# A decoder layer on one core: the last batch's linear attention moved ahead of an MLP tile, and the last tiles' turned values and down projections put in other banks

## The reference

```
i, f, g = x Wi^T, x Wf^T, x Wg^T
h[t] = sigmoid(f) h[t-1] + silu(i) (1 - sigmoid(f))          # a scan over tokens
x = layernorm(x + rmsnorm(h * silu(g)) Wo^T)
x = layernorm(x + wkv(w, u, k=x, v=ctx))                     # a linear attention: decayed sums of
                                                             # exp(k) v and exp(k) over past tokens
xq = quantise rows of x to 127 levels
hid = silu(xq Wgate^T) * (xq Wup^T)                          # 2 x 1408 columns
x = layernorm(x + quantise(hid) Wdown^T)                     # Wgate, Wup, Wdown quantised too
```

## Time and profile before

| | us |
|---|---|
| median of 3 runs (434.78 to 439.98) | 437.27 |
| the profiled execution | 435.36 |
| its span, first to last instruction | 433.4 |
| mean granted TensorE clock | 0.98 |

### The profile page before, as it was taken

How to read it: one execution, slowest core, us unless ns; L and a number is a source line. 1 busy time by engine, 2 the same in 40 slices (tenths; PEclk the granted TensorE clock), 3 DMA queues, 4 the chain that set the end, 5 groups by cost and what they waited for, 6 DMA issues and landing times.

```text
span 433.4 us, 7988 instructions
## 1 busy us (share of the span) xinstructions
PE 376.4 (87%) x2810; PEld 292.3 (67%) x2810; DVE 365.8 (84%) x620; ACT 320.0 (74%) x422; POOL 234.0 (54%) x282
## 2 busy tenths in 40 slices
PE   7799889789898899889997999899989997576872
PEld 7797889687865687659764976497648774232331
DVE  3889797575998799989898988898898989899584
ACT  3687777649827898588858995799668975985571
POOL 1775554542644844766475746594459436635451
PEclk9999999989999999999999999999999999889998
DMA  7946550662020010020203020302030202000101
GB/s 253 363 167 238 164 187 2 232 66 75 2 98 1 2 42 33 24 99 0 74 1 122 3 73 2 121 0 73 0 121 0 73 0 73 24 2 0 49 24 52
DMA packets 12843, 31.75 MB, mean 73 GB/s; under 512 B 2038, under 2 KB 5132, under 8 KB 12812
## 3 DMA queue, kind: packets, MB, share of 16 engines
q1 hardware_dynamic: 12812, 31.35, 21.9%
HBM read 27.14 MB, written 4.21 MB: 72 GB/s over the span
## 4 chain that ended last, share of the span: by engine, by line
ACT 22%; DVE 21%; PE 20%; issue 19%; POOL 12%; DMA 3%; SPq 1%; POOLq 0%; ACTq 0%; DVEq 0%
PE proj_ps L478 15%; POOL ring L1266 3%; PE slot_ps L579 2%; POOL x_low L1189 2%; ACT L978 2%; ACT hqT L943 2%; DVE inp L1459 2%; ACT ring L929 2%; ACT L982 2%; DVE stats L1486 2%; DMA ring<-w_gate_up_dram 2%; ACT turn_ps L883 2%; DMA ring<-w_down_dram 2%; POOL gate L1206 1%; DVE x_max L1575 1%
## 5 line engine op out<-in xcount | busy, mean ns | idle before, releaser
L579 PE MATMUL slot_ps<-w1q,xqT 128*128 128x512 bf16 (+1 forms) x384 | 83.1, 367 | 10.3 <-ACT xqT L920 7.6
L1266 POOL TENSOR_TENSOR ring<-ring 128x512 f32<-128x512 f32 (+1 forms) x48 | 60.5, 1262 | 25.7 <-ACT ring L929 25.7
L579 PEld LDWEIGHTS slot_ps<-w1q,xqT 128*128 128x128 bf16 x384 | 36.7, 99 | 48.7 <-issue 8.1
L478 PE MATMUL proj_ps<-x_high,proj_high 128*128 128x256 f32 x384 | 65.0, 291 | 5.0 <-DVE inp L1478 3.1
L478 PE MATMUL proj_ps<-x_low,proj_high 128*128 128x256 f32 x384 | 62.4, 284 | 0.0
L478 PE MATMUL proj_ps<-x_high,proj_low 128*128 128x256 f32 x384 | 62.0, 283 | 0.0
L478 PEld LDWEIGHTS proj_ps<-x_high,proj_high 128*128 128x128 f32 x384 | 53.4, 190 | 8.1 <-issue 7.1
L478 PEld LDWEIGHTS proj_ps<-x_low,proj_high 128*128 128x128 f32 x384 | 53.3, 191 | 0.0
L478 PEld LDWEIGHTS proj_ps<-x_high,proj_low 128*128 128x128 f32 x384 | 53.2, 190 | 0.0
L929 ACT ACTIVATE ring<-ring,zero_bias,x_scale 128x512 f32<-128x512 f32 (+1 forms) x48 | 36.9, 772 | 13.5 <-DVE ring L1598 13.4
L612 PE MATMUL slot_ps<-w2q,hqT 128*128 128x512 bf16 x176 | 42.5, 390 | 4.5 <-ACT hqT L943 3.5
(11 more groups left out here) (135 smaller groups left out, 849.5 us busy)
## 6 DMA issues: line engine op xcount, KB each, us to landing
ring<-w_gate_up_dram SPq DMA_DIRECT2D x11, 512.0 KB, 5.1
forget<-xT_dram SPq DMA_DIRECT2D x8, 512.0 KB, 3.8
x_sb<-x_dram SPq DMA_DIRECT2D x8, 512.0 KB, 4.0
c_sb<-cT_dram SPq DMA_DIRECT2D x8, 512.0 KB, 4.3
out_dram<-z SPq DMA_DIRECT2D x16, 256.0 KB, 2.1
ring<-w_down_dram SPq DMA_DIRECT2D x4, 704.0 KB, 5.4
scale_rows<-scratch_dram SPq DMA_DIRECT2D x2, 704.0 KB, 7.1
x<-wfT_dram SPq DMA_DIRECT2D x2, 512.0 KB, 5.7
```

What stands on the lines that cost most here:

```text
L478: last = nc.tensor.matmul(out, a, b, start=(i == 0), stop=(i == len(terms) - 1))
L579: last = nc.tensor.matmul(slot_ps[:, s, half * 512:half * 512 + width], xqT[:, par, d, t * P:(t + 1) * P], w1q[:, d, half * I + at:half * ...
L1266: nc.gpsimd.tensor_tensor(hid, hid, gate_buf[:, at:at + width], ALU.mult).then_inc(hid_ready, 1)
```

## The change

Three things are changed, all for n of 11 and more. In the loop nothing is.

- The linear attention of batch 7 stands further ahead in the lists of the four engines, and the MLP steps of tiles 12 and 13 further behind. On ACT its two visits to the exp table become one.
- The turned values of tiles 11 to 15 go to `proj_ps`, and the down projections of tiles 12 to 15 to `turn_ps`. The waits of `mlp_up`, `turn_hidden` and `mlp_down` follow from that.
- Tiles 13 and 15 keep their gate values in `forget` and `gate`; `scale_products` of tile n then waits for `hidden` of tile n-2, not n-1.

```diff
+TAIL = TILES - 5
+        def gate_part(n, c):
+            at, width = CHUNKS[c]
+            if isinstance(n, int) and n > TAIL and n % 2 == 1:
+                if c < 2:
+                    return forget[:, 2 * c:2 * c + 2, :].rearrange("p c t -> p (c t)")
+                return gate[:, 0:2, :].rearrange("p c t -> p (c t)")[:, 0:width]
+            return gate_buf[:, at:at + width]
+        def turned_hidden(n, t, part):
+            if isinstance(n, int) and n >= TAIL:
+                return proj_ps[:, part, 0:PARTS[part][1] * P // 2].bitcast(F16)
+            return part_16((t + 1 + NC) % 2, part)
+        def down_ps(n, t):
+            if isinstance(n, int) and n > TAIL:
+                return turn_ps[:, t * 512:t * 512 + D]
+            return slot_ps[:, (t + NC) % 2, 0:D]
...
             # mlp_up
-                        wait(pe, hq_ready, 2 * n - 2)
+                        if isinstance(n, int) and n > TAIL + 1:
+                            pe.wait_ge(mlp_read, (n - 1) * NC + 2)
+                        else:
+                            wait(pe, hq_ready, 2 * n - 2)
                     elif c == 1:
-                        wait(pe, down_read, n - 1)
+                        if isinstance(n, int) and n > TAIL + 2:
+                            pe.wait_ge(mlp_read, n * NC)
+                        else:
+                            wait(pe, down_read, n - 1)
...
             # turn_hidden
-                if isinstance(n, int) and n == TILES - 1:
-                    pe.wait_ge(down_read, n)
                 pe.wait_ge(hid_rounded, 2 * n + part + 1)
-                pe.wait_ge(mlp_read, chunks_read(n) - 1)
+                if isinstance(n, int) and n == TAIL:
+                    pe.wait_ge(z1_ready, TILES)
+                elif isinstance(n, int) and n > TAIL:
+                    pe.wait_ge(hq_ready, 2 * n + part - 1)
+                else:
+                    pe.wait_ge(mlp_read, chunks_read(n) - 1)
...
             # mlp_down
-                pe.wait_ge(mlp_read, chunks_read(n))
+                if isinstance(n, int) and n > TAIL:
+                    pe.wait_ge(xq_ready, BATCHES)
+                    wait(pe, down_read, n - 1 if n > TAIL + 2 else 0)
+                else:
+                    pe.wait_ge(mlp_read, chunks_read(n))
...
             # scale_products
-                        wait(dve, hid_ready, n * NC)
+                        if not isinstance(n, int) or n <= TAIL + 1:
+                            wait(dve, hid_ready, n * NC)
+                        elif n > TAIL + 2:
+                            dve.wait_ge(hid_ready, (n - 1) * NC)
                         wait(dve, hq_turned, 2 * n - 2)
...
             # vector list, tiles 14 and 15
             hidden_max_row(6, 1)
             hidden_scale(6, 0, 1)
-            layer_norm_3(12, 0)
-            scale_products(7, 0, [0])
-            scale_products(7, 0, [1])
             scale_products(7, 0, [2])
+            read_down(12, 6, 0)
+            scale_products(7, 1, [0])
+            scale_products(7, 1, [1])
             hidden_max_row(7, 0)
             hidden_scale(7, 1, 0)
+            layer_norm_3(12, 0)
+            scale_products(7, 1, [2])
+            hidden_max(7, 1, 0)
             read_down(13, 6, 1)
-            scale_products(7, 1, [0])
-            scale_products(7, 1, [1])
-            hidden_max(7, 1, 0)
-            scale_products(7, 1, [2])
-            layer_norm_3(13, 1)
             hidden_max(7, 1, 1)
             hidden_max(7, 1, 2)
             hidden_max_last(7, 1)
             hidden_scale(7, 1, 1)
+            layer_norm_3(13, 1)
             read_down(14, 7, 0)
...
             # pool list, the same tiles
-            residual_3(12, 0, 0)
             rstd_3(11, 1)
             hidden(7, 0, [0])
+            hidden(7, 0, [1])
+            residual_3(12, 0, 0)
+            hidden(7, 0, [2])
             rstd_3(12, 0)
-            hidden(7, 0, [1])
-            hidden(7, 0, [2])
+            hidden(7, 1, [0])
             residual_3(13, 0, 1)
-            hidden(7, 1, [0])
             hidden(7, 1, [1])
             hidden(7, 1, [2])
             rstd_3(13, 1)
```

More of the change, by code:

```diff
@@ L590, in turn_hidden @@
             def turn_hidden(n, t, part):
-                s = (t + 1 + NC) % 2
-                if isinstance(n, int) and n == TILES - 1:
-                    pe.wait_ge(down_read, n)
                 pe.wait_ge(hid_rounded, 2 * n + part + 1)
-                pe.wait_ge(mlp_read, chunks_read(n) - 1)
+                if isinstance(n, int) and n == TAIL:
[4 more added lines that the diff above has]
+                    pe.wait_ge(mlp_read, chunks_read(n) - 1)
                 first, count = PARTS[part]
                 for i in range(count):
-                    last = nc.tensor.transpose(part_16(s, part)[:, i * P:(i + 1) * P],
+                    last = nc.tensor.transpose(turned_hidden(n, t, part)[:, i * P:(i + 1) * P],
                                                low_halves(hid_buf(t)[:, (first + i) * P:
@@ L611, in mlp_down @@
                     for i in range(first, first + count):
-                        last = nc.tensor.matmul(slot_ps[:, s, 0:D], hqT[:, i, :], w2q[:, i, :],
+                        last = nc.tensor.matmul(down_ps(n, t), hqT[:, i, :], w2q[:, i, :],
                                                 start=(i == 0), stop=(i == IB - 1))
@@ L791, in _ @@
             mlp_up(7, 1, 0, [1])
+            turn_hidden(12, 0, 0)
+            turn_hidden(12, 0, 1)
             mlp_up(7, 1, 0, [2])
+            mlp_down(12, 0)
+            mlp_up(7, 1, 1, [0])
             turn_hidden(13, 1, 0)
             turn_hidden(13, 1, 1)
+            mlp_up(7, 1, 1, [1])
             mlp_down(13, 1)
-            mlp_up(7, 1, 1, [0])
-            mlp_up(7, 1, 1, [1])
             mlp_up(7, 1, 1, [2])
@@ L944, in read_hidden @@
                     hqT[:, first:first + count, :].rearrange("p i t -> p (i t)"),
-                    part_16((t + 1 + NC) % 2, part), ACT.Identity,
+                    turned_hidden(n, t, part), ACT.Identity,
                     bias=half_bias[:, :]).then_inc(hq_ready, 1)
@@ L1135, in _ @@
             exponential(7, 0)
+            round_hidden(11, 1, 0)
+            round_hidden(11, 1, 1)
             exponential(7, 1)
+            logarithm(7, 0)
+            reciprocal(7, 0)
+            read_hidden(11, 1, 0)
+            read_hidden(11, 1, 1)
+            logarithm(7, 1)
+            reciprocal(7, 1)
             silu_tables()
@@ L1139, in _ @@
             silu(6, 0, 0, [1])
-            round_hidden(11, 1, 0)
             silu(6, 0, 0, [2])
             normalise_3(10, 0)
-            round_hidden(11, 1, 1)
-            read_hidden(11, 1, 0)
-            read_hidden(11, 1, 1)
-            exp_tables()
-            logarithm(7, 0)
-            reciprocal(7, 0)
-            logarithm(7, 1)
-            reciprocal(7, 1)
-            silu_tables()
-            silu(6, 0, 1, [0])
+            silu(6, 0, 1, [0])
+            round_2(7, 1, 0)
+            round_2(7, 1, 1)
+            silu(6, 0, 1, [1])
+            read_inputs(7, 1)
+            silu(6, 0, 1, [2])
             round_hidden(12, 0, 0)
             round_hidden(12, 0, 1)
+            silu(7, 1, 0, [0])
             read_hidden(12, 0, 0)
             read_hidden(12, 0, 1)
-            silu(6, 0, 1, [1])
-            silu(6, 0, 1, [2])
-            round_2(7, 1, 0)
-            round_2(7, 1, 1)
-            read_inputs(7, 1)
+            silu(7, 1, 0, [1])
             normalise_3(11, 1)
+            silu(7, 1, 0, [2])
             round_hidden(13, 1, 0)
-            silu(7, 1, 0, [0])
             round_hidden(13, 1, 1)
-            silu(7, 1, 0, [1])
+            silu(7, 1, 1, [0])
             read_hidden(13, 1, 0)
+            read_hidden(13, 1, 1)
+            silu(7, 1, 1, [1])
             normalise_3(12, 0)
-            silu(7, 1, 0, [2])
-            read_hidden(13, 1, 1)
             round_hidden(14, 0, 0)
-            silu(7, 1, 1, [0])
-            silu(7, 1, 1, [1])
+            silu(7, 1, 1, [2])
             round_hidden(14, 0, 1)
-            silu(7, 1, 1, [2])
             read_hidden(14, 0, 0)
@@ L1388, in _ @@
             past_values(7, 0)
+            rstd_3(10, 0)
             past_values(7, 1)
-            rstd_3(10, 0)
+            newton(7, 0)
+            newton(7, 1)
+            first_token(7)
             hidden(6, 0, [0])
@@ L1393, in _ @@
             hidden(6, 0, [2])
-            first_token(7)
-            newton(7, 0)
-            newton(7, 1)
-            hidden(6, 1, [0])
             residual_3(11, 1, 1)
             rstd_2(7)
+            hidden(6, 1, [0])
             hidden(6, 1, [1])
             hidden(6, 1, [2])
-            residual_3(12, 0, 0)
             rstd_3(11, 1)
             hidden(7, 0, [0])
+            hidden(7, 0, [1])
+            residual_3(12, 0, 0)
+            hidden(7, 0, [2])
             rstd_3(12, 0)
-            hidden(7, 0, [1])
-            hidden(7, 0, [2])
```

(2 more changed lines are left out.)

35 lines of the change are left out of this document (15 added, 20 removed).

## The result

| | before | after |
|---|---|---|
| median us | 436.43 (4 runs, 434.78 to 439.98) | 450.0 (4 runs, 447.56 to 452.13) |
| profiled execution's span | 433.4 | 445.8 |
| tail: start of tile 11's maximum to the last norm's end | 65.0 | 77.9 |

The ratio is 1.030, 95% interval 1.025 to 1.035: 13.6 us slower. The direction was forecast, the size (7.5 us, range up to 448.6) was too small. The loss is in the tail: in the two traces it is 12.9 us longer. The traced execution of the changed kernel is the quickest of its four (447.56 us, mean granted clock 0.972, the others 0.957 to 0.964), so the clock may cost more in the median than the trace shows. The part ahead of it is the same program, yet the tail's start moves between 365.2 and 368.9 us over the profiled executions of this study.

What follows compares the result with a forecast made beforehand. It took DVE's list to bound the tail up to 399.4 us, then a chain of hand-overs. Terms -5.3, +9.7 and +3.1 for the clock gave +7.5 on 437.3, so 444.8 us, range 439.5 to 448.6.

Steps and rivals of the forecast that it cites:

- Part one: Linear attention of batch 7: values turned 2.9 us earlier, inverse scale 3.8 us earlier, PE starting tile 14 at 395.5.
- Part two: Tiles 14 and 15: first product at 399.7 against 402.78, then 11.1 us to marker two, which comes 5.3 us earlier.
- marker two: The end of tile 15's second chunk on DVE, at 416.17 us before and forecast at 410.9.
- Part three: Marker two to the last norm's end: hand-overs between engines take 24.2 us against 14.5, 9.7 us more.
- Each of its steps: Seven hand-overs on DVE, POOL and ACT, from tile 14's maximum to the end: 3.25 + 2.4 + 1.4 + 3.5 + 1.5 + 2.8 + 9.3.
- Part four: PE's clock falling to 1.2 GHz in the tail: half of two possible costs together, 3.1 us.
- Both falls that were priced: Half clock at tile 14's two first chunks, 0 to +3.5 us, and at tile 15's transposes and down projection, 0 to +2.7.
- a sign: Named beforehand as showing the forecast: the clock at 0.50 somewhere between 383 and 399, and after 421.
- the one that hand-overs would bind in one place only: Tile 13's down projection reading or tile 12's norm doesn't bind; 2 to 4 us less, +1 left, 438.3; chance 0.1.
- The faster one: Slots were the bound: marker two 5.3 us earlier, the tail behind it keeps 14.5 us, 431.6; chance 0.06.
- a clock no worse than before: Hand-overs as forecast in the tail without added clock cost: +4.4 us, 441.7; chance 0.2.

Runs made afterwards that it cites:

- The experiment with the two apart: Changed kernel with tile 13's first two products moved on DVE behind batch 7's normalising and scale, away from POOL's product beside it: 450.94 us, 1.031.
- moving the three DVE steps: Changed kernel with tile 12's norm, the reading of tile 13's down projection and tile 13's norm moved earlier on DVE: 441.26 us, 1.012.
- the three single moves: Changed kernel with tile 12's norm, the reading of tile 13's down projection or tile 13's norm alone earlier on DVE: 446.2, 448.3 and 446.1 us.
- the banks would bring something: The change's other banks and second gate buffer alone, in the order of the kernel before: 436.17 us against 436.58, 0.999.

## Why the prediction was wrong in size

- **Part one, the linear attention 3.8 us earlier: failed.** The values were turned 0.6 us earlier where 2.9 were forecast, and the inverse scale is out at 30.1 us where it was at 30.2 before. I gave the moved DVE instructions the time that they had taken in the kernel before, most of it beside an idle POOL. Moved, three of them start while POOL works, and the three groups take 2.5 us more than before. The experiment with the two apart shows the cause for the normalising; for the scans and numerators it is read from the traces, in which they are short wherever POOL is not in a product. Another 0.9 us is the turning of the values at half clock (1.97 us instead of 1.09), which counts with the clock below, and 0.4 lies between `residual_2` and the normalising. The trace of before had the collisions: its 32 numerators take 645 ns on average over the launch, and 470 in the tail.

```profile
L1526 DVE SCALAR_TENSOR_TENSOR num<-num,bonus_col,p_state 128x255 f32<-128x255 f32 x32 | 18.8, 645 | 0.0
```

- **Part two, tile 14 and 15 to marker two: right at full clock.** From tile 14's first product to marker two 11.2 us, 11.1 forecast, 13.4 before. The product's wait for tile 12's transposes is there, 5.2 us long. It comes late by part one and by the clock: marker two is 1.2 us later than before and not 5.3 earlier.
- **Part three, marker two to the end: right.** 26.2 us; the forecast was 24.2 without the clock. The last down projection has 1.4 of the difference. Each of its steps is in the chain above, and moving the three DVE steps won 7.3 us, 5.9 of it without the clock.
- **Part four, the clock: too small.** Both falls that were priced came, and I took half of the two together, 3.1 us. The clock cost 3.5 us up to marker two, as much as the bound, and 1.4 of the 2.7 at the end: 4.9. Some 0.9 of the 3.5 is at the turned values, where I had named a fall as a sign but given it no price.

The sum by what was measured: -5.3 (parts one and two as forecast, at full clock) + 2.5 (collisions) + 3.5 and 1.4 (clock) + 9.7 (hand-overs) = +11.8, against +12.9 in the trace; 1.1 is left unnamed, about half on either side of marker two. Of the 5.4 us between +7.5 and +12.9, then, 2.5 are collisions, 1.8 the clock and 1.1 unnamed. The failed step is the first: the term for the linear attention had no price for POOL's work beside it. With both clock falls and without collisions the sum is +9.3, at 446.6 inside my range; with the collisions it is 449.1, half a microsecond outside. The clock's term was the second mis-sized one. A small slip besides: 0.62 and two thirds of 0.2 make 0.75 for "slower by more", where I wrote 0.77.

The Trainium skill's rule that I had weighed (TensorE: Matmul & The Clock Gate, HAM oscillation), half the throttled time, gives (6.8 + 6.8 + 3.4 + 3.4) / 2 = 10.2 us for the stretches of the changed tail down to 437.8 as an estimate; the runs show 4.9 on the path. Part of the throttled time again lay in stretches in which nobody waited for PE.

Of the rivals, the one that hand-overs would bind in one place only is refuted by the three single moves, each of which wins 1.5 to 1.9 us up to tile 15's rounding. The faster one is refuted, and so is a clock no worse than before. That the banks would bring something is true of the trace alone: 1.6 us, not told from nothing in the runs.

## What to carry to other kernels

When lists of several engines are reordered, look at what each short step of an old tile now stands behind, on every engine that it visits: a norm of 1 us behind a later tile's product held up three engines here, and three such moves on one engine were worth 8.7 us, some 6 of them as hand-overs and the rest as clock. Take a duration for a moved instruction from places where the other engines do what they will do beside it, and look for the same line elsewhere in the trace with a longer time. A plan that gathers the vector work leaves PE idle, and the first matmuls behind that belong in the sum at half clock.

## What was not expected of the hardware

Three kinds of DVE instruction here, all with their operands in SBUF, end only after POOL's instruction when they start inside one of 384 or 512 columns: the numerators and the normalising 0.28 us after it, the scans of `num` 0.55. In the tail of the changed kernel that made 1.48 us of 0.47, 1.51 of 0.54 and 1.69 of 0.67, and the normalising is back to 0.54 when the product is moved away. The launch of the kernel before shows the same: its 7 numerators that start inside such a POOL instruction take 1.22 to 1.49 us and the other 25 take 0.45 to 0.48; 6 of its 16 normalising instructions start inside one and take 1.50 to 1.67, the others 0.54 to 0.55. Where DVE's instruction started first and POOL's came during it, DVE's kept its time.

Having everything in SBUF is not enough for it. The statistics of the norms (`stats<-z`, one large input) that start inside a POOL instruction keep their 0.67 to 0.69 us, and the row maximum its 1.62. Those with an operand in PSUM (`divide`, `refine`, the products from the slots) kept their 0.68 us beside POOL. Which property of the three kinds decides was not tried.
